# A graph network on one core: bucketed groups ordered in the first convolution go from 96 to 128, gathered groups of the first and third from 92 and 64 to 64 and 20

## The chip, the cores and the metric

One Trainium2 chip, one of its cores. The metric is the device time of one execution in microseconds (us). The kernel was written by hand, engine by engine, with its own semaphores; nothing is scheduled by a compiler.

## What is computed

A graph of 12,500 nodes with 32 features and 200,000 edges that come sorted by destination. First a layer of edge messages: each edge takes the 32 features of its source (`h`, a layer norm with a ReLU), a small network of the edge's weight and its direction, and the messages are summed by destination. Then three graph convolutions with widths 32, 128 and 32:

```
def _gcn_conv(x, src, dst, norm, W, b, n_nodes):
    h = x @ W
    msg = h[src] * norm[:, None]
    out = jax.ops.segment_sum(msg, dst, num_segments=n_nodes)
    return out + b
...
h = jnp.maximum(_layernorm(x, axis=-1), 0.0)
x = x + _L0_gnn_ref(h, edge_weight, edge_attr_3, edge_index, ...)
h = jnp.maximum(_layernorm(x, axis=-1), 0.0)
h = relu(_gcn_conv(h, src, dst, norm, W1, b1, n))
h = relu(_gcn_conv(h, src, dst, norm, W2, b2, n))
h = relu(_gcn_conv(h, src, dst, norm, W3, b3, n))
x = x + h
```

What costs time is `h[src]` followed by the sum over `dst`, four times over the 200,000 edges.

## The kernel before

The stages run one after the other, each after a table of node rows has been written to HBM: layer 0 (0 to 2664 us of the profile), preparation, the first convolution from 2771 us (called conv1), the second from about 4080 us (conv2), the third from 5526 us (conv3). Each has two ways of doing an edge, and splits its edges between them.

**A gathered group** is 1024 edges. POOL issues eight indirect DMAs (`gathers`, L782), each of 128 rows of the table, and behind each a memset of a scrap tile, 128x512 (`pause_between`, L762), for which the next gather waits (`made`). PE multiplies the rows by a one-hot matrix (L2153, `gathered_sum`, in eight matmuls for the convolutions), DVE adds the sum to the accumulator (L1766) and makes the next one-hot (L1657). Four groups can be in flight (`rows`), a buffer comes free when its sum has been made. Layer 0 gathers all of its 196 groups (`NG`).

**A bucketed group** is 1408 edges, ordered beforehand by the block of 128 nodes that the source lies in. It is done in `NCK` = 5 chunks, without any gather: the table lies in SBUF, and a chunk picks rows by matmuls with a one-hot of the sources. A chunk is: mark the sources (conv3: DVE L1613, `mark_sources`; conv1: ACT in two steps, L985 `near` and L994, for four chunks of five, and DVE L1613 for the fifth), PE `take` L2067 (20 matmuls), ACT `copy_bucket` L1007 (PSUM to SBUF), DVE `mark_destinations` L1642, PE `give` L2085 (5 matmuls). Each half of the marks waits until the take two chunks earlier is done (`bucket_taken`). Once for each group there is DVE `pair_destinations` L1624, DVE `add_bucket` L1726, and ACT's DMA `load_places` L968, 800 KB from HBM spread over all partitions, two groups ahead in conv3 (issued behind the last chunk's copy), one group ahead in conv1.

**Ordering.** Where an edge of a bucketed group belongs is found once, in conv1, for all groups that any convolution buckets (`NBG` = 96); the result goes to `places_d` in HBM and `dst_at` in SBUF, and conv2 and conv3 reuse it. One ordering is: DVE `count_blocks` L1543 to L1551, PE `count_prefix` L2040 (11 matmuls), ACT `copy_prefix` L976, DVE `rank_edges` L1557 to L1566, DVE `set_values` L1574 to L1580, PE `place_values` L2049 (44 matmuls), DVE `keep_places` L1587 to L1593, ACT's DMA `store_places` L958. Its parts are laid between the chunks of conv1 by hand: `parts_in(k, last)` says which part of which ordering goes with chunk k.

Tables of numbers set the mix: `GATHERED` gives the gathered groups of each stage, `LOOP` the gathered and bucketed groups of one iteration of each stage's loop, `REST` those of its last iteration. Before, conv1 gathers 92 groups and buckets 76 (380 chunks), conv2 100 and 70, conv3 64 and 96 (480 chunks). An iteration of conv1 has 50 chunks and 12 orderings (`RANKS`); an ordering takes four chunks there, and three in the last iteration, with parts in this order:

```
def parts_in(k, last):
    if last:
        return [divmod(k, 3)]
    return [(k // 4, (0, None, 1, 2)[k % 4])]
```

Two of the orderings stand ahead of conv1.

Of the kernel before, what the change touches and what calls it, by code (L numbers as in the profile page):

```python
# [27 lines left out]
P = 128  # L28
# [11 lines left out]
UNROLL = 4  # L40
# [27 lines left out]
GATHERED = [NG, 92, 100, 64]  # L68
LOOP = [(UNROLL, 0), (12, 10), (12, 8), (8, 12)]
REST = [(UNROLL, 0), (8, 6), (16, 14), (8, 12)]  # L70
# [21 lines left out]
RANKS = 12  # L92
# [15 lines left out]
assert RANKS % SLOTS == 0 and 4 * RANKS + 2 <= LOOP[1][1] * NCK and OWN_LAST == REST[1][1] - 2  # L108
assert OWN_LAST <= RANKS_LAST and 3 * RANKS_LAST == REST[1][1] * NCK

# [23 lines left out]
def gnn_kernel(nc, x, src, dst, edge_attr, edge_weight, w1, b1, w2, b2,  # L134
               W1, B1, W2, B2, W3, B3, out):
    ctx = ExitStack()
    with ctx:
# [59 lines left out]
        shared = sb("shared", [P, 5792])  # L197
        hid = shared[:, 0:1024].rearrange("p (s q e) -> p s q e", s=2, q=TPG // 2)
# [13 lines left out]
        odd_src = shared[:, 896:896 + NBG * BJ]  # L212
        odd_dst = shared[:, 2016:2016 + NBG * BJ]
# [18 lines left out]
        thirds1 = arena[:, 4208:4208 + NB * F3 // 2].bitcast(bf16).rearrange("p (b f) -> p b f", f=F3)  # L232
        thirds3 = arena[:, :].bitcast(bf16).rearrange("p (b f) -> p b f", f=2 * HID)[:, :, 0:F3]
        thirds = [None, thirds1, None, thirds3]
        src_b = arena[:, 8912:8912 + NBG * BJ].bitcast(i32)
        dst_b = arena[:, 9968:9968 + NBG * BJ].bitcast(i32)
        dst_b_rows = arena[0:NBG, 11024:11024 + BE].bitcast(i32)
        start_b = arena[:, 12432:12432 + NBG].bitcast(i32)
        src_place = arena[:, 9968:9968 + NBG * BJ].bitcast(bf16).rearrange("p (e two) -> p e two", two=2)
        dst_b_near = arena[:, 11024:11024 + NBG * BJ].bitcast(bf16).rearrange("p (e two) -> p e two", two=2)  # L240
        part_a = arena[:, 0:NBG * BJ].bitcast(i32)
        part_b = arena[:, 1120:1120 + NBG * BJ].bitcast(i32)
        near = arena[:, 1120:1120 + NBG * BJ]
# [288 lines left out]
        def parts_in(k, last):  # L532

            if last:
                return [divmod(k, 3)]
            return [(k // 4, (0, None, 1, 2)[k % 4])]
# [278 lines left out]
        def _(act):  # L815
# [201 lines left out]
            def conv(n):  # L1017

                def body(step, first, last):
                    groups, chunks_, starts_at = shape(n, last)  # L1020
                    u = -1
                    for k in range(chunks_):
# [15 lines left out]
                        for i, part in parts:  # L1038
                            if part == 1 and not last and i < RANKS:
                                copy_prefix(step, i)  # L1040
# [6 lines left out]
                        for i, part in parts:  # L1047
                            if part == 1 and last:
                                copy_prefix(step, i)
                            if part == (2 if last else None) and 0 < i <= (RANKS_LAST if last else RANKS):  # L1050
                                store_places(step, i - 1, last)
# [1231 lines left out]
```

How the kernel before makes its waits and increments, by code:

```python
        @block.sync  # L583
        def _(sp):
            for h, lo, hi in ((0, 0, 96), (0, 96, NB), (1, 0, 96), (1, 96, NB - 1)):
                sp.dma_start(dst_rows[lo:hi, h, :],
                             dst[(h * NB + lo) * GE:(h * NB + hi) * GE].rearrange("(g e) -> g e", e=GE)).then_inc(rows_in, 16)
            for at, n in ((0, ETAIL), (ETAIL, HALF - ETAIL), (HALF, HALF)):
                sp.dma_start(dst_rows[NB - 1:NB, 1, at:at + n],
                             dst[E - n:E].rearrange("(g e) -> g e", g=1)).then_inc(rows_in, 16)
            sp.dma_start(xn[:, 0:NB - 1, :], x[0:NCOL, :].rearrange("(p b) f -> p b f", p=P)).then_inc(x_in, 16)
            sp.wait_ge(pads, 1)
            sp.dma_start(xn[0:N - NCOL, NB - 1, :], x[NCOL:N, :]).then_inc(x_in, 16)
            def groups_of(lo, hi):
                return edge_attr[lo * GE:hi * GE, :].rearrange("(g e) c -> g (e c)", e=GE)
            for h, lo, hi in ((0, 0, 96), (0, 96, NB), (1, 0, 96)):
                sp.dma_start(attr_rows[lo:hi, h, :], groups_of(h * NB + lo, h * NB + hi)).then_inc(edges_in, 16)
            sp.wait_ge(pads, 2)
            sp.dma_start(attr_rows[96:NB - 1, 1, :], groups_of(NB + 96, NG - 1)).then_inc(edges_in, 16)
            sp.dma_start(attr_rows[NB - 1:NB, 1, 0:3 * ETAIL],
                         edge_attr[(NG - 1) * GE:E, :].rearrange("(g e) c -> g (e c)", g=1)).then_inc(edges_in, 16)
            sp.wait_ge(made, 9)
            sp.wait_ge(meta_ready, 2)
```

## Time and profile before

| | us |
|---|---|
| median of 3 runs (6437.45 to 6447.65) | 6441.06 |
| the profiled execution | 6419.31 |
| its span in the trace | 6417.5 |
| conv1, first to last `take` | 2770.7 to 3994.0 |
| conv3, first to last `take` | 5526.0 to 6391.9 |

Busy time over the span: POOL 5536.7 us (86%), PE 4556.8 (71%), DVE 3632.7 (57%), ACT 2714.1 (42%). The shares are averages over stages with different limits, so the views by stage and the single rows of a timeline say more. In a timeline a row is the start in us, the length in us, the engine, the line of the kernel, the operation with its tiles, and in brackets how long the engine had stood idle before it and what released it.

### The profile page before, as it was taken

What the parts mean: (1) busy time and instruction counts of PE and PEld (TensorE: products, weight loads), DVE (VectorE), ACT (ScalarE), POOL (GpSimd) and SP (SyncE); (2) the same over time, 40 slices, a digit from 0 to 9 for tenths busy, and PEclk for the clock granted to TensorE, in tenths of its full rate; (3) what the DMA queues carried; (4) which work ended last, traced back from release to release, by engine and by line L of the source; (5) the groups of instructions that cost most, each with busy time, mean ns of one, the idle gap of its engine ahead of it and who ended that gap; (6) DMA issues with size and microseconds to landing.
All of it is one profiled execution on the core that took longest, in us unless ns stands there. A gap on an engine that the chain in (4) does not pass through costs nothing.

```text
span 6417.5 us, 179150 instructions
## 1 busy us (share of the span) xinstructions
PE 4556.8 (71%) x62463; PEld 3336.9 (52%) x62464; DVE 3632.7 (57%) x8469; ACT 2714.1 (42%) x6550; POOL 5536.7 (86%) x7276
## 2 busy tenths in 40 slices
PE   4777777777777777655555555888888889766666
PEld 3444444444444444444444444777777778455554
DVE  7666666666666666755555555333333333544445
ACT  4444444444444444365555554333333344433332
POOL 7888888888888888588888887798888898688887
PEclk9888888888888888755555555888888899655555
DMA  3111111111111111332222222322222222433333
GB/s 79 31 30 30 30 30 30 30 30 30 30 30 30 30 30 30 34 75 69 64 69 69 69 69 70 96 81 76 81 81 76 81 81 85 118 105 109 110 107 98
DMA packets 494970, 400.88 MB, mean 62 GB/s; under 512 B 269575, under 2 KB 454828, under 8 KB 493537
## 3 DMA queue, kind: packets, MB, share of 16 engines
q10 hardware_dynamic: 146996, 207.67, 9.8%
q0 software_dynamic: 115712, 109.02, 9.7%
q1 hardware_dynamic: 231536, 74.48, 5.4%
q8 instruction: 459, 7.52, 0.5%
q14 instruction: 267, 2.19, 0.1%
HBM read 375.52 MB, written 15.29 MB: 61 GB/s over the span
## 4 chain that ended last, share of the span: by engine, by line
POOL 59%; issue 35%; POOLq 2%; PE 2%; DVE 1%; DMA 1%; ACT 0%; DVEq 0%; SPq 0%; ACTq 0%
POOL pause L762 31%; POOL rows L782 28%; POOLq L761 2%; PE radial L2209 0%; DMA table<-arena 0%; PE radial L2067 0%; PE radial L2222 0%; PE psX L2082 0%; POOLq L760 0%; PE sums L2153 0%; DMA rows<-table,idx 0%; DMA xn<-in_x 0%; DVE rows L1827 0%; PE radial L2008 0%; ACT rows L1103 0%
## 5 line engine op out<-in xcount | busy, mean ns | idle before, releaser
L782 POOL DMA_INDIRECT rows<-table,idx x3616 | 3535.1, 978 | 794.6 <-POOL pause L762 484.5
L762 POOL MEMSET pause<- 128x512 f32 x3616 | 1983.8, 549 | 2.5
L2067 PE MATMUL radial<-arena,shared 128*32 128x96 bf16 (+1 forms) x31200 | 1021.7, 277 | 198.9 <-issue 95.2
L1942 PEld LDWEIGHTS sums<-scratch,onehot 128*64 128x64 f32 x9408 | 791.4, 147 | 492.6 <-issue 205.5
L1942 PE MATMUL sums<-scratch,onehot 128*64 128x264 f32 (+1 forms) x9408 | 1009.1, 362 | 25.2 <-DVE scratch L1377 14.1
L2067 PEld LDWEIGHTS radial<-arena,shared 128*32 128x32 bf16 (+1 forms) x31200 | 719.2, 119 | 378.5 <-issue 169.5
L1007 ACT CAST scratch<-radial 128x480 bf16<-128x480 f32 x860 | 477.6, 557 | 985.4 <-PE radial L2067 750.1
L1924 PE MATMUL radial<-shared 64*128 64x384 bf16 x1568 | 296.8, 370 | 704.5 <-DVE scratch L1360 590.9
L1927 PE MATMUL radial<-shared 64*128 64x384 f32 x3136 | 785.6, 582 | 0.0
L2153 PE MATMUL sums<-onehot,rows 128*128 128x80 f32 (+1 forms) x2844 | 402.3, 314 | 515.8 <-DMA rows<-table,idx 489.2
L1360 DVE TENSOR_TENSOR scratch<-radial,shared 128x768 f32<-128x768 f32 x784 | 743.6, 949 | 0.0
L1613 DVE TENSOR_SCALAR shared<-scratch,line 128x640 bf16<-128x640 bf16 (+1 forms) x906 | 455.3, 503 | 480.5 <-PE radial L2067 387.4
L880 ACT COPY shared<-rows 128x192 f32<-128x192 f32 x196 | 89.3, 456 | 1494.4 <-DMA rows<-table,idx 1493.1
L2153 PEld LDWEIGHTS sums<-onehot,rows 128*128 128x128 f32 (+1 forms) x2844 | 365.5, 223 | 569.0 <-issue 566.2
L850 ACT ACTIVATE dist<-iota,rel 128x64 f32<-128x64 f32 (+1 forms) x2368 | 620.3, 344 | 34.4 <-issue 31.9
L1326 DVE TENSOR_TENSOR shared<-arena,rows 128x576 f32<-128x576 f32 x196 | 148.7, 759 | 755.6 <-ACT shared L887 446.7
L1766 DVE TENSOR_TENSOR accT<-accT,sums 96x80 f32 (+1 forms) x256 | 60.3, 236 | 897.1 <-PE sums L2153 723.9
L1924 PEld LDWEIGHTS radial<-shared 64*128 64x128 bf16 x1568 | 82.4, 95 | 931.2 <-issue 711.3
L1352 DVE TENSOR_TENSOR scratch<-radial,shared 128x512 f32<-128x512 f32 x784 | 535.3, 683 | 13.4 <-issue 13.4
L1003 ACT COPY scratch<-radial 128x384 f32<-128x384 f32 x350 | 167.8, 480 | 589.7 <-PE radial L2067 585.3
L1642 DVE TENSOR_TENSOR shared<-radial,shared 128x480 bf16<-128x480 bf16 x860 | 344.0, 401 | 50.1 <-PE psT L2085 17.6
L1927 PEld LDWEIGHTS radial<-shared 64*128 64x128 f32 x3136 | 337.9, 222 | 36.9 <-issue 31.0
(237 smaller groups left out, 6075.3 us busy)
## 6 DMA issues: line engine op xcount, KB each, us to landing
scratch<-places_d ACTq DMA_DIRECT2D x242, 800.0 KB
rows<-table,idx POOLq DMA_INDIRECT x3616
shared<-in_edge_weight SPq DMA_DIRECT2D x390, 128.0 KB
idx<-in_src SPq DMA_DIRECT2D x451, 4.0 KB
table<-arena SPq DMA_DIRECT2D x24, 256.0 KB, 2.5
table<-arena SPq DMA_DIRECT2D x2, 1176.0 KB, 10.6
accT<-in_edge_attr SPq DMA_DIRECT2D x2, 1152.0 KB
table<-arena SPq DMA_DIRECT2D x24, 96.0 KB, 2.0
```

The lines of the kernel that those rows point to most:

```text
L762: nc.gpsimd.memset(pause[:, :], 0.0).then_inc(made, 1)
L782: (pool.indirect_dma_start(rows_3[:, r, j, :] if n in (1, 3) else rows[:, r, j, 0:WIDTH[n]], None, tables[n], bass.IndirectOffsetOnAxis(ap ...
L850: ins = nc.scalar.activation(dist[:, j, 0:span], iota[:, 0:span], ACT.Abs, scale=-1.0, bias=rel[:, bass.ds(step.tile(u) + j, 1)])
L1007: nc.scalar.copy(taken[n][:, h, :, :], radial[0][:, h, 0:KC * F3].rearrange("p (t f) -> p t f", f=F3)).then_inc(bucket_copied, 1)
L1352: prod = v.tensor_tensor(msg[:, h, t:t + 2, 0:2 * SEG0].rearrange("p t (m s) -> p t m s", s=16), R[:, :, 0:256].rearrange("p t (m s) -> p ...
L1360: last = v.tensor_tensor(msg[:, h, t:t + 2, SEG0 + 16 * (MUL + 1):TAIL0].rearrange("p t (n s) -> p t n s", s=16), R[:, :, 256:384].unsquee ...
L1613: v.tensor_scalar(from_src[n][:, k % 2, :, :, :], places[v_ % 2][:, :, c * KC * CAP:(c + 1) * KC * CAP].rearrange("p i (t r) -> p i t r", ...
L1924: nc.tensor.matmul(radial[q % 2][:, k, 0:RDIM], ones_h[half, :], bias_rows[half, :], start=True, stop=False, tile_position=(k * HID0, 0))
L1927: last = nc.tensor.matmul(radial[q % 2][:, k, 0:RDIM], hid[half, u % 2, q, :], w2n[half, 0, :], start=False, stop=True, tile_position=(k * ...
L1942: last = nc.tensor.matmul(there, onehot[:, u % 2, 4 * h + t, 0:SW], taken_from, start=(h + q + part == 0), stop=(h == 1 and q == 1 and par ...
L2067: last = nc.tensor.matmul(d, from_src[n][:, h, i, t, :], table_of(n, s), start=True, stop=True, tile_position=(0, 32 * i))
L2153: mm = nc.tensor.matmul(sums[0:w, u % 2, 0:CWIN], far_rows[j], (onehot if n == 2 else onehot_3)[0:counts[j], u % 2, j, 0:CWIN], start=(j = ...
```

## The change

1. The third convolution gathers 20 groups and buckets 128 (640 chunks), in 5 iterations, not 8: 160 gathers in it for 512.
2. The first convolution gathers 64 groups and buckets 96 (480 chunks): 512 gathers for 736. All 3616 gathers become 3040. Layer 0 and the second convolution keep their numbers.
3. `NBG` follows the largest number of buckets: 128 groups are ordered, 126 of them within conv1 (before 94). Every iteration now uses the order that the last one had, an ordering in three chunks with a part in each; an iteration of conv1 has 60 chunks and 16 orderings, the last one 14 orderings in 60 chunks. 378 of the 480 chunks carry a part.
4. ACT's `copy_prefix` stands behind the copy of its chunk in all iterations; before, it stood between the two marking steps in all but the last.
```diff
-GATHERED = [NG, 92, 100, 64]
-LOOP = [(UNROLL, 0), (12, 10), (12, 8), (8, 12)]
-REST = [(UNROLL, 0), (8, 6), (16, 14), (8, 12)]
+GATHERED = [NG, 64, 100, 20]
+LOOP = [(UNROLL, 0), (8, 12), (12, 8), (4, 26)]
+REST = [(UNROLL, 0), (8, 12), (16, 14), (4, 24)]
...
-RANKS = 12
+RANKS = 16
...
+        bucket_edges = sb("bucket_edges", [P, 2 * NBG * BJ])
...
-        odd_src = shared[:, 896:896 + NBG * BJ]
-        odd_dst = shared[:, 2016:2016 + NBG * BJ]
+        odd_src = shared[:, 1024:1024 + NBG * BJ]
+        odd_dst = bucket_edges[:, NBG * BJ:2 * NBG * BJ]
...
         def parts_in(k, last):
 
-            if last:
-                return [divmod(k, 3)]
-            return [(k // 4, (0, None, 1, 2)[k % 4])]
+            return [divmod(k, 3)]
...
                         parts = parts_in(k, last) if n == 1 else []
-                        for i, part in parts:
-                            if part == 1 and not last and i < RANKS:
-                                copy_prefix(step, i)
                         if n == 1 and more and (k + 1) % NCK != NCK - 1:
                             mark_sources(step, k + 1)
                         copy_bucket(n, step, k)
...
                         for i, part in parts:
-                            if part == 1 and last:
+                            if part == 1 and i < (RANKS_LAST if last else RANKS):
                                 copy_prefix(step, i)
-                            if part == (2 if last else None) and 0 < i <= (RANKS_LAST if last else RANKS):
+                            if part == 2 and 0 < i <= (RANKS_LAST if last else RANKS):
                                 store_places(step, i - 1, last)
...
-    nc = bacc.Bacc("TRN2", target_bir_lowering=False, num_devices=1)
+    nc = bacc.Bacc("TRN2", target_bir_lowering=False, num_devices=1, dynamic_dma_scratch_size=4096)
```

How the instructions move is shown for two engines in the first loop body of conv1. ACT before, over the four chunks of one ordering (`places_d` holds the places in HBM, `scratch<-radial 128x480` is the copy of a chunk, `arena<-radial 128x104` is `copy_prefix`):

```order
L968 DMA scratch<-places_d 128x4x800 [waits places_out1]
L985 ACTIVATE shared<-scratch,line 128x640 [waits bucket_taken]
L976 CAST arena<-radial 128x104 [waits prefix_made]
L994 ACTIVATE shared<-shared,one 128x640 [waits from_src_near]
L1007 CAST scratch<-radial 128x480 [waits bucket_summed,bucket_taken] x2
L985 ACTIVATE shared<-scratch,line 128x640 [waits bucket_taken,places_in1]
L994 ACTIVATE shared<-shared,one 128x640 [waits from_src_near]
L1007 CAST scratch<-radial 128x480 [waits bucket_summed,bucket_taken]
L985 ACTIVATE shared<-scratch,line 128x640 [waits bucket_taken]
L994 ACTIVATE shared<-shared,one 128x640 [waits from_src_near]
L1007 CAST scratch<-radial 128x480 [waits bucket_summed,bucket_taken]
L958 DMA places_d<-src_at 128x32 [waits src_at_made]
```

ACT in the change, over the three chunks of one ordering (its lines are one lower):

```order
L1006 CAST scratch<-radial 128x480 [waits bucket_summed,bucket_taken]
L967 DMA scratch<-places_d 128x4x800 [waits places_out1]
L984 ACTIVATE shared<-scratch,line 128x640 [waits bucket_taken]
L993 ACTIVATE shared<-shared,one 128x640 [waits from_src_near]
L1006 CAST scratch<-radial 128x480 [waits bucket_summed,bucket_taken]
L975 CAST arena<-radial 128x104 [waits prefix_made]
L1006 CAST scratch<-radial 128x480 [waits bucket_summed,bucket_taken]
L957 DMA places_d<-src_at 128x32 [waits src_at_made]
L984 ACTIVATE shared<-scratch,line 128x640 [waits bucket_taken,places_in1]
L993 ACTIVATE shared<-shared,one 128x640 [waits from_src_near]
L1006 CAST scratch<-radial 128x480 [waits bucket_summed,bucket_taken]
```

`copy_prefix` went from between the two marking steps to behind the copy of its chunk, and the store of the places comes once in three copies, not once in four.

DVE before, from `count_blocks` to the start of `rank_edges` (L1642 is `mark_destinations`, once for each chunk):

```order
L1543 TENSOR_TENSOR arena<-radial,arena 128x1144 [waits places_summed]
L1546 TENSOR_TENSOR arena<-arena 128x121
L1549 TENSOR_TENSOR arena<-arena 128x121 [waits ranking]
L1551 TENSOR_REDUCE arena<-arena 128x11 [waits ranking]
L1642 TENSOR_TENSOR shared<-radial,shared 128x480
L1642 TENSOR_TENSOR shared<-radial,shared 128x480 [waits bucket_summed]
L1557 TENSOR_TENSOR arena<-arena 128x1144 [waits prefix_copied]
```

DVE in the change (its lines are four lower):

```order
L1539 TENSOR_TENSOR arena<-radial,arena 128x1144 [waits places_summed]
L1542 TENSOR_TENSOR arena<-arena 128x121
L1545 TENSOR_TENSOR arena<-arena 128x121 [waits ranking]
L1547 TENSOR_REDUCE arena<-arena 128x11 [waits ranking]
L1638 TENSOR_TENSOR shared<-radial,shared 128x480 [waits bucket_summed,dst_paired]
L1553 TENSOR_TENSOR arena<-arena 128x1144 [waits prefix_copied]
```

One chunk's `mark_destinations` now stands between the two steps, where there were two.

## Rows read from the trace of the kernel before

**Rows 1.** Windows: layer 0, conv1, conv3; length, busy of each engine, PEclk, DMA.

```profile
95.00:2664.00 2569.00, 1884.34 (x14035) 1158.29 (x14033) 1790.78 (x3460) 1055.89 (x3074) 2300.09 (x3071) 0.88 0.17 31
2735.00:3997.00 1262.00, 707.17 (x15491) 543.78 (x15489) 728.10 (x2413) 711.52 (x1093) 1114.99 (x1472) 0.52 0.27 67
...
5520.00:6390.00 870.00, 581.96 (x12453) 449.37 (x12452) 429.32 (x1339) 268.78 (x484) 777.19 (x1016) 0.52 0.38 106
```

**Rows 2.** Timeline of POOL in layer 0, two gathers, a pause left out.

```profile
395.78 0.95 POOL L782 DMA_INDIRECT rows<-table,idx  x1 [0.16 <-POOL pause L762]
...
398.76 1.06 POOL L782 DMA_INDIRECT rows<-table,idx  x1 [1.48 <-issue]
```

**Rows 3.** The chain between 230 and 900 us: start, us, what.

```profile
397.28 1.26 issue
...
557.65 1.27 issue
```

**Rows 4.** Waits of conv3 for gathered rows: us in total, times, longest.

```profile
PE sums L2153 <- DMA rows<-table,idx: 99.4, 40, 6.6
```

**Rows 5.** One line, the takes of conv1, then of conv3: count, first and last start.

```profile
L2067 PE MATMUL radial<-arena,shared x7600: 202/281/281, 2770.7 to 3994.0; 128*32 128x96 bf16 x195
...
L2067 PE MATMUL radial<-arena,shared x9600: 202/281/281, 5526.0 to 6391.9; 128*32 128x96 bf16 x196
```

**Rows 6.** Timeline of ACT in conv3, while POOL gathers.

```profile
5916.10 0.56 ACT L1007 CAST scratch<-radial 128x480 bf16<-128x480 f32 x1 [1.12 <-PE radial L2067]
5917.78 0.56 ACT L1007 CAST scratch<-radial 128x480 bf16<-128x480 f32 x1 [1.12 <-PE radial L2067]
5919.45 0.56 ACT L1007 CAST scratch<-radial 128x480 bf16<-128x480 f32 x1 [1.11 <-PE radial L2067]
```

**Rows 7.** Timeline of POOL over the same time.

```profile
5915.53 0.55 POOL L762 MEMSET pause<- 128x512 f32 x1
...
5917.32 0.54 POOL L762 MEMSET pause<- 128x512 f32 x1
...
5918.99 0.54 POOL L762 MEMSET pause<- 128x512 f32 x1
```

**Rows 8.** Timeline of PE in conv3, when POOL has ended its last gather.

```profile
6387.31 0.59 PE L2067 MATMUL radial<-arena,shared 128*32 128x96 bf16 x20
...
6388.39 0.59 PE L2067 MATMUL radial<-arena,shared 128*32 128x96 bf16 x20
...
6391.08 0.40 PE L2067 MATMUL radial<-arena,shared 128*32 128x96 bf16 x20
...
6391.76 0.40 PE L2067 MATMUL radial<-arena,shared 128*32 128x96 bf16 x20
```

**Rows 9.** Groups of conv3 by line and form, DVE: count, busy, mean ns.

```profile
L1613 DVE TENSOR_SCALAR shared<-scratch,line 128x640 bf16<-128x640 bf16 x478 | 204.6, 428 | 212.2 <-PE radial L2067 152.2 <-remote 44.8 <-issue 12.4
L1642 DVE TENSOR_TENSOR shared<-radial,shared 128x480 bf16<-128x480 bf16 x477 | 191.0, 400 | 33.0 <-PE psT L2085 17.6 <-PE psX L2085 12.2 <-remote 2.9
```

**Rows 10.** Timeline of ACT in conv1, a load of places and who waits for it.

```profile
3489.27 0.41 ACTq L968 DMA_DIRECT2D scratch<-places_d  x1
...
3493.47 0.83 ACT L985 ACTIVATE shared<-scratch,line 128x640 bf16<-128x640 bf16 x1 [0.38 <-DMA scratch<-places_d]
```

**Rows 11.** Timeline of DVE in conv1, last iteration: starts of orderings.

```profile
3897.36 0.74 DVE L1543 TENSOR_TENSOR arena<-radial,arena 128x1144 bf16<-128x1144 bf16 x1
...
3904.76 0.75 DVE L1543 TENSOR_TENSOR arena<-radial,arena 128x1144 bf16<-128x1144 bf16 x1
...
3917.97 0.75 DVE L1543 TENSOR_TENSOR arena<-radial,arena 128x1144 bf16<-128x1144 bf16 x1
...
3926.67 0.75 DVE L1543 TENSOR_TENSOR arena<-radial,arena 128x1144 bf16<-128x1144 bf16 x1
```

**Rows 12.** Timeline of ACT in conv1, two copies with no ordering between them.

```profile
2797.41 0.56 ACT L1007 CAST scratch<-radial 128x480 bf16<-128x480 f32 x1
...
2799.47 0.54 ACT L1007 CAST scratch<-radial 128x480 bf16<-128x480 f32 x1
```

More of the change, by code:

```diff
@@ L107 @@
 RANKS_LAST = OWN_LAST + OTHERS - (RANKS - OWN) * (ITS[1] - 1)
-assert RANKS % SLOTS == 0 and 4 * RANKS + 2 <= LOOP[1][1] * NCK and OWN_LAST == REST[1][1] - 2
-assert OWN_LAST <= RANKS_LAST and 3 * RANKS_LAST == REST[1][1] * NCK
+assert RANKS % SLOTS == 0 and 3 * RANKS + 3 <= LOOP[1][1] * NCK and OWN_LAST == REST[1][1] - 2
+assert OWN_LAST <= RANKS_LAST and 3 * RANKS_LAST <= REST[1][1] * NCK
 NORM0 = sqrt(4 * pi) / sqrt(2 * MUL)
@@ L229, in gnn_kernel @@
         taken = [None, taken_3, taken_w, taken_3]
-        thirds1 = arena[:, 4208:4208 + NB * F3 // 2].bitcast(bf16).rearrange("p (b f) -> p b f", f=F3)
+        thirds1 = arena[:, 4320:4320 + NB * F3 // 2].bitcast(bf16).rearrange("p (b f) -> p b f", f=F3)
         thirds3 = arena[:, :].bitcast(bf16).rearrange("p (b f) -> p b f", f=2 * HID)[:, :, 0:F3]
         thirds = [None, thirds1, None, thirds3]
[L235 to L240, printed above, removed]
+        src_b = bucket_edges[:, 0:NBG * BJ].bitcast(i32)
+        dst_b = arena[:, 9600:9600 + NBG * BJ].bitcast(i32)
+        dst_b_rows = arena[0:NBG, 11008:11008 + BE].bitcast(i32)
+        start_b = arena[:, 12416:12416 + NBG].bitcast(i32)
+        src_place = arena[:, 9600:9600 + NBG * BJ].bitcast(bf16).rearrange("p (e two) -> p e two", two=2)
+        dst_b_near = arena[:, 11008:11008 + NBG * BJ].bitcast(bf16).rearrange("p (e two) -> p e two", two=2)
         part_a = arena[:, 0:NBG * BJ].bitcast(i32)
-        part_b = arena[:, 1120:1120 + NBG * BJ].bitcast(i32)
-        near = arena[:, 1120:1120 + NBG * BJ]
+        part_b = arena[:, 1408:1408 + NBG * BJ].bitcast(i32)
+        near = arena[:, 1408:1408 + NBG * BJ]
         in_block = arena[:, 0:BJ * NCODE // 2].bitcast(bf16).rearrange("p (j c) -> p j c", j=BJ)
@@ L1055, in body @@
                             load_places(n, step, v + 2)
-                    if last and n == 1:
+                    if last and n == 1 and 3 * RANKS_LAST + 2 >= chunks_:
                         store_places(step, RANKS_LAST - 1, last)
@@ L1778, in body @@
                             ranking(step, k, last)
-                    if last and n == 1:
+                    if last and n == 1 and 3 * RANKS_LAST >= chunks_:
                         keep_places(step, RANKS_LAST - 1, last)
@@ L2182, in body @@
                         turn_given(step, chunks_ // NCK - 1)
-                    if last and n == 1:
+                    if last and n == 1 and 3 * RANKS_LAST >= chunks_:
                         place_values(step, RANKS_LAST - 1)
```

## The prediction, made before the changed kernel had run

> **What bounds the kernel now.** I cut the span into its stages first, with the windows, since the page's shares average over them. In layer 0 POOL is busy 2300 of 2569 us, in conv1 1115 of 1262, in conv3 777 of 870 [rows 1]. POOL's timeline gives its beat: a gather of 0.95 us, 0.16 us of idle time ahead of it [rows 2], and a pause memset of 0.54. In conv3 the pauses start 1.79 and 1.67 us apart [rows 7]; over the stage 1.69 us (866 us for 512 gathers), 13.5 for a group of eight. Every 96th gather is late: POOL stands idle for 1.48 us where it stands 0.16 otherwise [rows 2], and the chain shows two such stretches of 1.27 us 160.3 us apart, which is 96 beats [rows 3]. In conv3 PE waits for gathered rows 40 times, 99.4 us in all [rows 4]. So conv1 and conv3 cost what their gathers cost: conv3's takes span 5526.0 to 6391.9, 866 us for 512 gathers; conv1's 2770.7 to 3994.0, 1223 us for 736 [rows 5].
>
> The second thing to see is the pace of a bucketed chunk. While POOL gathers, conv3's copies start 1.68 and 1.67 us apart [rows 6], and each starts just when a pause memset ends on POOL: 5915.53 plus 0.55 is 5916.08, the copy starts at 5916.10; 5917.32 plus 0.54 is 5917.86, copy 5917.78; 5918.99 plus 0.54 is 5919.53, copy 5919.45 [rows 7]. I read this as a lock: the end of a take becomes visible once in a beat of POOL. When POOL has issued its last gather the takes follow one another in 1.08 us with matmuls at the half clock (0.59 us a take) and then in 0.68 us at 0.40 us a take [rows 8]. The clock granted over conv1 and conv3 is 0.52 of full speed, so nearly always the 1.2 GHz level; in layer 0 it is 0.88 [rows 1].
>
> **The change, part by part.** Durations are those of the profiled execution, 6419.3 us; the median shown is 21.8 us above it, so the sum is a difference, added to 6441.06.
>
> **conv3.** It loses 352 gathers and gets 160 chunks. 20 groups at 13.5 us keep POOL busy for 270 us. In that time chunks go at 1.69 us: 160 chunks. The other 480 run unlocked. Their lower bound is the tail's fastest pace, taken as 0.76 (a little over the 0.68 seen) [rows 8]; the upper is its cold pace, 1.09. Two more floors lie between. DVE needs 0.43 for the marks of the sources and 0.40 for those of the destinations [rows 9], 0.83 us, and two small operations for each group (some 0.25 us each, over five chunks) make it about 0.92 us a chunk. And the load of places (L968): in conv1 one was issued at 3489.27 and its user released at 3493.47, 4.2 us [rows 10]. In conv3 it is issued behind the last copy of one group and used six takes later; with mark and take some 5.5 us in six chunks, 0.92 us again. I take **1.0 us**: both floors, and a clock that is high most of the time. 270 + 480 = 750 us for 866: **-116**. Ends: at 0.76 635 us, -231; at 1.09 793 us, -73. The waits for rows of gathers should go, since a group then comes every 32 chunks and four can be in flight.
>
> **conv1.** It loses 224 gathers, gets 100 chunks and 32 orderings. 64 groups at 13.5 us are 864 us, so POOL no longer sets its length: the chunks with their orderings do. The new order is the one that the last iteration had, so its rows price it: `count_blocks` starts at 3897.36 and again at 3904.76, 7.4 us, with no gather waited for; 3917.97 to 3926.67, 8.7 us, holds a wait for one [rows 11]. I take 8.0 us, between them. 126 orderings are 1008 us. The other 102 chunks go at ACT's pace, two copies 2.06 us apart [rows 12], 209 us. 1217 for 1223: -6. In the order of ACT, `copy_prefix` moves behind a copy, some 1.4 us later than between the marks; DVE has one `mark_destinations` between `count_blocks` and `rank_edges` in place of two. Both are within the last iteration's rows already. The tables for 128 groups make preparation a little longer, DVE operations of a third more columns ahead of the first chunk; I put +3. Together **-3**; ends 7.4 us (-79) and 8.7 us (+85).
>
> **Descriptor scratch.** It is a quarter. If the late gather every 96th is the recycling of this space, it comes every 24th. Where POOL bounds (layer 0 and conv2, 2368 gathers) there were 24 such stalls of 1.32 us, 32 us. Four times as many at a quarter of the length each is **0**; at the same length, 72 more, +95; if a short one hides in the 0.16 us between, -32. Elsewhere POOL has slack, and it costs nothing.
>
> **Layer 0, conv2, the tables between:** not touched, 0. Sum: -116 - 3 + 0 = **-119**, 6441 - 119 = **6322 us**.
>
> **The rivals.**
>
> *A: the stall keeps its length.* For it: its length is the same to 0.01 us both times [rows 3], as a fixed piece of work or a wait for one landing would be. Against it: a walk over 96 entries would be constant too. +95: 6417 us, within a few us of the edge of no change.
>
> *B: the clock stays at 1.2 GHz in conv3.* For it: 0.52 over the stage [rows 1], and 1.08 us between takes in each burst before the clock rises. Against it: PE had waits in nearly every chunk there, and it rose after PE had run three takes without one [rows 8]. 270 + 523 = 793 us, so -73 and -3: 6365 us. The Trainium skill (TensorE: Matmul & The Clock Gate, "What's actually happening") says that the default is throttled and that activity releases it; by that rule B falls, the trace's tail agrees with it (0.59 us a take becomes 0.40), and the forecast stands.
>
> *C: the ordering in each chunk is the new chain of conv1, and B holds too.* An ordering runs through DVE, PE, ACT, DVE, PE and DVE again, each step behind a chunk's own work. If three chunks need 8.7 us always [rows 11], conv1 is +85; with -73 the sum is +12: 6453 us, near no change, and with part of A's 95 clearly slower. It decides from 8.6 us an ordering.
>
> *D, the other side: the pace of 1.69 us is the chunk's own.* The place is the loop take, copy, give, marks of conv3; the lock to POOL would be by chance of equal lengths. For it: 1.68 us stands in every row of the stage [rows 6], and gathers that wait for sums could take their beat from the chunks. Against it: the tail's 1.08 and 0.68 [rows 8]. Price: 640 x 1.69 = 1082 us for 866, +216, with conv1's -3: 6654 us. It decides from a pace of 1.35 us, where 640 chunks last 866. A rule speaks on its side. The Trainium skill (SBUF — State Buffer, "Who interferes with whom") says that PE and ACT never wait on anyone; by it POOL's work could not hold back the end of a take, and the time would be D's 6654. The rows of POOL and ACT side by side [rows 6, 7] are against the rule here, as far as three beats can be.
>
> **How the numbers follow.** Forecast as it stands 0.43, A 0.24, B 0.14, C 0.11, D 0.08. A measurement of this kernel tells about 0.2%, 13 us, from no change. Faster: the forecast, B, and 0.14 of A: 0.71. Same: 0.06, of A. Slower: D, C, and 0.04 of A: 0.23. The range goes from 6200, the forecast with conv3 at its warm pace (-118), to 6540, C with the whole of A's 95; outside lie D and the lowest corner of all ends.
>
> **What would show it.** In the changed kernel's profile: 3040 gathers; conv3's takes spanning about 750 us; copies 1.69 us apart only while POOL has gathers and about 1.0 apart else; PEclk high in conv3; waits of PE for gathered rows near nothing; POOL idle in conv3 two thirds of the time. conv1's takes spanning about 1217 us with `count_blocks` every 8.0 us. Late gathers every 24th, of 0.3 us each beyond the 0.16. The forecast is wrong if copies of conv3 stay 1.6 us apart with POOL idle (D), if late gathers keep 1.48 us (A), if takes stay at 0.59 us (B), if conv1 is over 1290 us long (C).

## The result, and the profile after

The changed kernel takes **6186.68 us** (median of 4 runs, 6179.96 to 6193.57); the kernel before, timed beside it, 6439.26 us (4 runs). The ratio is **0.9608, 95% interval 0.9591 to 0.9626**, so 252.6 us less, where 119 were forecast (6322, range 6200 to 6540). The direction was right, the size less than half, and the time lies below the range.

The page of the changed kernel (its profiled execution took 6193.57 us), with the span, the busy times, three rows of the slices and the shares of the chain by engine and by line:

```profile
span 6191.7 us, 194777 instructions
...
PE 4635.9 (75%) x70151; PEld 3410.8 (55%) x70152; DVE 3941.3 (64%) x9309; ACT 2973.3 (48%) x7002; POOL 4661.6 (75%) x6124
...
PE   4777777777777777756666666788888888988787
...
POOL 7999999999999999947666666298988889863330
PEclk9888888888888888865555555688888889988877
...
POOL 40%; issue 27%; DVE 11%; PE 10%; DMA 6%; ACT 2%; POOLq 1%; DVEq 1%; SPq 0%; ACTq 0%
POOL pause L761 21%; POOL rows L781 19%; DMA scratch<-places_d 5%; PE radial L2063 3%; PE radial L2036 2%; DVE arena L1553 1%; PE psX L2081 1%; PE psT L2081 1%; PE radial L2045 1%; POOLq L760 1%; DVE arena L1539 1%; DVE arena L1556 1%; DVE arena L1560 1%; DVE shared L1609 1%; DVE shared L1638 1%
```

POOL is at 4661.6 us where it was at 5536.7; its digits are still 9 in layer 0 and mostly 8 and 9 in the second convolution, and they fall to 3 and 0 in the last four slices, the third convolution. The clock row, 5 in those slices before, is now at 8 and 7. The windows of layer 0, the first and the third convolution, to lay beside [rows 1]:

```profile
95.00:2664.00 2569.00, 1899.03 (x14187) 1167.19 (x14186) 1807.82 (x3499) 1057.67 (x3088) 2296.30 (x3075) 0.89 0.17 31
2740.00:3960.00 1220.00, 811.98 (x19444) 640.56 (x19444) 911.48 (x2985) 869.26 (x1374) 747.96 (x994) 0.51 0.29 80
5480.00:6170.00 690.00, 560.66 (x16168) 426.62 (x16172) 522.06 (x1599) 357.41 (x641) 238.30 (x308) 0.81 0.49 159
```

In the third convolution PE is busy 561 of 690 us and DVE 522; POOL only 238. The granted clock is 0.81 of full speed where it was 0.52. The first convolution stays at 0.51. The takes of the first and then of the third convolution, beside [rows 5]:

```profile
L2063 PE MATMUL radial<-arena,shared x9600: 206/281/281, 2747.5 to 3952.8; 128*32 128x96 bf16 x196
```

```profile
L2063 PE MATMUL radial<-arena,shared x12800: 202/206/281, 5481.9 to 6165.5; 128*32 128x96 bf16 x197
```

By these rows the stages compare as follows. The last column is the prediction's term.

| from first to last take, us | before | after | measured | forecast |
|---|---|---|---|---|
| all ahead of the first convolution | 2770.7 | 2747.5 | -23.2 | +3 |
| first convolution | 1223.3 | 1205.3 | -18.0 | -6 |
| from there to the third | 1532.0 | 1529.1 | -2.9 | 0 |
| third convolution | 865.9 | 683.6 | -182.3 | -116 |
| sum over the spans (with the last 26 us) | 6417.5 | 6191.7 | -225.8 | -119 |

The spans differ by 226 us and the medians by 253: the profiled execution of before was 20 us faster than the median of its runs, that of after 7 us slower. So 107 us of the forecast's error lie in the stages, and 27 in which execution was profiled. Of the 107, 66 are the third convolution's, 26 lie ahead of the first (layer 0's gathers alone span 26.6 us less, 2605.7 for 2632.3), 12 in the first and 3 between it and the third.

Layer 0's gathers, at the place where one stood idle for 1.48 us before [rows 2]:

```profile
396.03 0.95 POOL L781 DMA_INDIRECT rows<-table,idx  x1 [0.16 <-POOL pause L761]
...
397.68 0.95 POOL L781 DMA_INDIRECT rows<-table,idx  x1 [0.16 <-POOL pause L761]
...
399.33 0.95 POOL L781 DMA_INDIRECT rows<-table,idx  x1 [0.16 <-POOL pause L761]
```

There is no late gather any more: beyond the first 32 of layer 0's 1568 gathers the old trace has one every 96th, 15 of them (the expectations below say 16), that starts 2.98 us after the one before it, 1.33 us more than the median beat. Over the whole kernel there are 31, 15 in layer 0 and 6, 6 and 4 in the convolutions. The new trace has none. And the waits of the third convolution, beside [rows 4]:

```profile
ACT scratch L1006 <- PE radial L2063: 314.9, 531, 5.2
POOL rows L781 <- PE sums L2149: 279.9, 13, 27.2
...
DVE shared L1609 <- DMA scratch<-places_d: 60.4, 66, 2.7
...
PE sums L2149 <- DMA rows<-table,idx: 1.0, 1, 1.0
```

PE waits once, 1.0 us, for gathered rows (40 times, 99.4 us before). POOL waits instead, 280 us in 13 stretches, for sums that free its buffers. New is a wait of DVE for the loads of places, 66 times, 60 us.

The last thing is the pace of a chunk. Copies of the third convolution in the changed kernel, and POOL's gathers over the same time:

```profile
5658.24 0.56 ACT L1006 CAST scratch<-radial 128x480 bf16<-128x480 f32 x1 [2.62 <-PE radial L2063]
...
5659.35 0.56 ACT L1006 CAST scratch<-radial 128x480 bf16<-128x480 f32 x1 [0.55 <-PE radial L2063]
5660.44 0.56 ACT L1006 CAST scratch<-radial 128x480 bf16<-128x480 f32 x1 [0.53 <-PE radial L2063]
5661.61 0.56 ACT L1006 CAST scratch<-radial 128x480 bf16<-128x480 f32 x1 [0.61 <-PE radial L2063]
```

```profile
5658.01 0.95 POOL L781 DMA_INDIRECT rows<-table,idx  x1 [0.16 <-POOL pause L761]
...
5659.72 0.96 POOL L781 DMA_INDIRECT rows<-table,idx  x1 [0.16 <-POOL pause L761]
...
5661.38 0.95 POOL L781 DMA_INDIRECT rows<-table,idx  x1 [0.16 <-POOL pause L761]
```

POOL is gathering, and the copies come 1.11, 1.09 and 1.17 us apart, at no fixed place of its beat (5658.24 is 0.23 us behind the start of a gather, 5659.35 is 1.34 behind it, 5660.44 is 0.72 behind the next). Counted over the stage, the takes follow one another in 1.07 us on average while POOL gathers (235 of them) and in 1.07 us while it doesn't (404). The 1.69 us that the prediction charged to 160 chunks don't exist here.

### The profile page after: what moved, and what is told of

Read it like the earlier page. It is cut to its first block, busy times and chain, and to the rows that moved or that the text cites. A ratio compares the mean times of both kernels' runs of the same rounds, so it can differ in the third digit from the quotient of the medians.

```text
span 6191.7 us, 194777 instructions
## 1 busy us (share of the span) xinstructions
PE 4635.9 (75%) x70151; PEld 3410.8 (55%) x70152; DVE 3941.3 (64%) x9309; ACT 2973.3 (48%) x7002; POOL 4661.6 (75%) x6124
## 4 chain that ended last, share of the span: by engine, by line
POOL 40%; issue 27%; DVE 11%; PE 10%; DMA 6%; ACT 2%; POOLq 1%; DVEq 1%; SPq 0%; ACTq 0%
POOL pause L761 21%; POOL rows L781 19%; DMA scratch<-places_d 5%; PE radial L2063 3%; PE radial L2036 2%; DVE arena L1553 1%; PE psX L2081 1%; PE psT L2081 1%; PE radial L2045 1%; POOLq L760 1%; DVE arena L1539 1%; DVE arena L1556 1%; DVE arena L1560 1%; DVE shared L1609 1%; DVE shared L1638 1%
## 5 line engine op out<-in xcount | busy, mean ns | idle before, releaser
L781 POOL DMA_INDIRECT rows<-table,idx x3040 | 2944.3, 969 | 1308.1 <-PE sums L2149 607.3
L761 POOL MEMSET pause<- 128x512 f32 x3040 | 1698.7, 559 | 1.7
L2063 PE MATMUL radial<-arena,shared 128*32 128x96 bf16 (+1 forms) x36400 | 1062.6, 263 | 333.3 <-ACT shared L993 164.9
L1006 ACT CAST scratch<-radial 128x480 bf16<-128x480 f32 x1120 | 618.4, 552 | 421.9 <-PE radial L2063 407.6
L1609 DVE TENSOR_SCALAR shared<-scratch,line 128x640 bf16<-128x640 bf16 (+1 forms) x1086 | 570.0, 525 | 263.2 <-PE radial L2063 164.0
L1348 DVE TENSOR_TENSOR scratch<-radial,shared 128x512 f32<-128x512 f32 x784 | 535.0, 682 | 13.7 <-issue 13.5
L1638 DVE TENSOR_TENSOR shared<-radial,shared 128x480 bf16<-128x480 bf16 x1120 | 448.4, 400 | 96.0 <-PE psX L2081 44.0
L2149 PE MATMUL sums<-onehot,rows 128*128 128x80 f32 (+1 forms) x2272 | 337.1, 319 | 210.4 <-DMA rows<-table,idx 195.3
L2149 PEld LDWEIGHTS sums<-onehot,rows 128*128 128x128 f32 (+1 forms) x2272 | 308.7, 227 | 248.4 <-issue 242.1
L1762 DVE TENSOR_TENSOR accT<-accT,sums 128x80 f32 (+1 forms) x184 | 43.2, 235 | 610.1 <-PE sums L2149 601.2
L984 ACT ACTIVATE shared<-scratch,line 128x640 bf16<-128x640 bf16 x384 | 318.1, 828 | 83.3 <-DMA scratch<-places_d 57.5
```

The source lines that it names most:

```text
L761: nc.gpsimd.memset(pause[:, :], 0.0).then_inc(made, 1)
L781: (pool.indirect_dma_start(rows_3[:, r, j, :] if n in (1, 3) else rows[:, r, j, 0:WIDTH[n]], None, tables[n], bass.IndirectOffsetOnAxis(ap ...
L1006: nc.scalar.copy(taken[n][:, h, :, :], radial[0][:, h, 0:KC * F3].rearrange("p (t f) -> p t f", f=F3)).then_inc(bucket_copied, 1)
L1348: prod = v.tensor_tensor(msg[:, h, t:t + 2, 0:2 * SEG0].rearrange("p t (m s) -> p t m s", s=16), R[:, :, 0:256].rearrange("p t (m s) -> p ...
L1609: v.tensor_scalar(from_src[n][:, k % 2, :, :, :], places[v_ % 2][:, :, c * KC * CAP:(c + 1) * KC * CAP].rearrange("p i (t r) -> p i t r", ...
L1638: v.tensor_tensor(by_twos(to_dst[n][:, k % 2, :, :]), row_pairs(iota1_ps, KC), in_pairs(dst_pair[:, v_ % 2, c * KC:(c + 1) * KC, :], BWIN) ...
```

## The experiments

Three things were to be explained: why chunks beside gathers are no longer slow, where the late gathers went, and how much of the gain is the scratch, the first and the third convolution. The theories at the start were S, that the smaller descriptor scratch did both of the first two, and M, that the mix of groups did. The runs are called e1 to e13 (there is no e4), as in the expectations. All ratios are to the kernel before, timed beside each run; e6, e7 and e9 were executed once each.

### The scratch alone

```diff
-    nc = bacc.Bacc("TRN2", target_bir_lowering=False, num_devices=1)
+    nc = bacc.Bacc("TRN2", target_bir_lowering=False, num_devices=1, dynamic_dma_scratch_size=4096)
```

> The kernel before with the descriptor scratch of the change (4096), nothing else. Theory S (the scratch did it): the late gathers of every 96th (1.48 us of idle time) are gone in all stages, as in the changed kernel, which is 16 x 1.33 us in layer 0 and 8 x 1.3 in the second convolution, and the copies of the third convolution follow their takes within 0.1 us, where they came 0.3 to 1.6 us late; as POOL still bounds each stage the time falls by about 30 to 45 us, to some 6400. Theory M (the mix did it, the scratch does nothing): the profile is that of before, late gathers and late copies included, 6440. Rival A of the prediction (the stall comes four times as often at its full length): 6535.

Measured (e1): 6385.5 us for 6428.8, ratio 0.9930 (0.9913 to 0.9947). The late gathers are gone in all stages, layer 0's gathers span 2605.6 us (before 2632.3, after 2605.7). In the third convolution 337 of 474 copies beside gathers start within 0.1 us of their take's last matmul and none later than 0.3, where the trace of before had 32 of 471 within 0.1 us and 269 over 1.3 us late. That looked like theory S in full, though the stage was only 7.6 us shorter (858.4). The time fits the stalls: 31 x 1.33 = 41 us, measured 43. Rival A is out: no stall came back more often.

### Size of the scratch or place of the tiles

```diff
+        room = sb("room", [P, 3072])
         accT = sb("accT", [P, NPAD + WIN])
...
+    nc = bacc.Bacc("TRN2", target_bir_lowering=False, num_devices=1, dynamic_dma_scratch_size=4096)
```

> The kernel before with the descriptor scratch at 4096, as in e1, and an unused tile of 12,288 bytes for each partition ahead of all others, so that every tile lies where it lay before. If the size of the scratch is what counts, the run is e1's: copies of the third convolution within 0.3 us of their takes, no gather late every 96th, 6385 us. If it was the place of the tiles, the copies are 0.3 to 1.6 us late as before and the time is 6430.

Measured (e5): 6385.4 us, ratio 0.9927 (0.9910 to 0.9943), copies on time, no late gather. So where the tiles lie shows no effect; the size of the scratch takes the late gathers away. (The copies need more than that, see below.) How it goes with the size was tried with 8192 on the kernel before:

> The kernel before with half of its descriptor scratch (8192). With 16384 layer 0 has 16 late gathers, 96 apart, each 1.33 us longer than the median; with 4096 and 2048 it has none. If the late gather is the reuse of the whole scratch and each quarter of it hides in the beat, half of it may show as gathers 48 apart, up to 33 of them of 0.5 us or less extra: 6385 to 6405. If the length of a late gather doesn't depend on the size, it comes twice as often: 33 of 1.33 us in layer 0, 6455. If it is only 16384 that has it, 6385 and no gather over 2.2 us beyond the first 32.

e12 took 6384.0 us, ratio 0.9921 (0.9905 to 0.9938), and in layer 0 no two gathers start over 2.2 us apart beyond the first 32. Of the sizes 16384, 8192 and 4096 only the first has late gathers. They don't scale with the size, and what they are stays open. Then the changed kernel, with only the size set to 2048:

> The changed kernel with half of its descriptor scratch (2048 for 4096). If a smaller scratch only makes the recycling finer, so that each piece hides behind the pause, the time stays at 6187 and no gather is late. If the scratch holds too few descriptors for the gathers that are in flight, POOL waits at each of them for a landing: gathers of layer 0 come more than 1.65 us apart and the time is over 6250.

e2 took 6173.3 us, ratio 0.9598 (0.9582 to 0.9614) against the kernel before, where the changed kernel had 0.9608 with an overlapping interval: no difference shown, layer 0 the same to 1 us.

### The state that the prediction summed

The third convolution beside few gathers, with the full scratch and then with the small one. Both leave out 44 gathered groups of it:

```diff
-GATHERED = [NG, 92, 100, 64]
-LOOP = [(UNROLL, 0), (12, 10), (12, 8), (8, 12)]
-REST = [(UNROLL, 0), (8, 6), (16, 14), (8, 12)]
+GATHERED = [NG, 92, 100, 20]
+LOOP = [(UNROLL, 0), (12, 10), (12, 8), (4, 20)]
+REST = [(UNROLL, 0), (8, 6), (16, 14), (4, 16)]
...
-E0 = GATHERED[3] * GE
+E0 = 64 * GE
...
-BUCKETED = [0] + [NBG - (GATHERED[n] * GE - E0) // BE for n in (1, 2, 3)]
+BUCKETED = [0] + [NBG - (GATHERED[n] * GE - E0) // BE for n in (1, 2)] + [NBG]
```

> The kernel before, full scratch, with the third convolution at 20 gathered and 96 bucketed groups; the other 44 gathered groups are left out, their edges are not computed. This is the state that the prediction summed, 480 chunks beside 160 gathers with the full scratch. By the prediction's terms 160 chunks go at 1.69 us while POOL gathers and 320 at 1.0: its takes span 590 us, with the copies late while POOL gathers and on time else. If the pace of 1.69 us is the chunks' own (rival D) they span 810 us. If the full scratch does no harm to a stage that is not bound by gathers, they span 480 x 1.07 = 513 us.

> e6 with the scratch at 4096, the same 44 gathered groups of the third convolution left out. With the pace of the changed kernel, 683.5 us for 640 chunks, its takes span 513 us, all copies within 0.3 us of their takes. The difference to e6 is what the full scratch costs a stage whose gathers do not bound it: 77 us by the prediction's terms, 0 if late copies cost nothing there.

Their takes, in e6 and then in e7:

```profile
L2067 PE MATMUL radial<-arena,shared x9600: 202/206/281, 5551.7 to 6046.4; 128*32 128x96 bf16 x196
```

```profile
L2067 PE MATMUL radial<-arena,shared x9600: 202/206/281, 5510.8 to 6010.3; 128*32 128x96 bf16 x196
```

Measured: **494.7 us with the full scratch (e6), 499.6 with the small one (e7)**, for 480 chunks. Neither 590 nor 810; 1.03 and 1.04 us a chunk, with 1.02 and 1.03 beside gathers, and all but three of the 960 copies within 0.3 us of their takes. The full scratch doesn't slow the chunks. That is against theory S: the first convolution of this kernel is the same program as before, with the same scratch, and there 140 of 371 copies beside gathers are within 0.1 us, where the trace that I had read has 8 of 373.

### The first convolution with both scratches

Once with the changed kernel's code and scratch (e3: the third convolution back at 64 and 96, 96 groups ordered), once the same with the tiles and the scratch of before (e8). The edit of e3, against the changed kernel:

```diff
-GATHERED = [NG, 64, 100, 20]
-LOOP = [(UNROLL, 0), (8, 12), (12, 8), (4, 26)]
-REST = [(UNROLL, 0), (8, 12), (16, 14), (4, 24)]
+GATHERED = [NG, 64, 100, 64]
+LOOP = [(UNROLL, 0), (8, 12), (12, 8), (8, 12)]
+REST = [(UNROLL, 0), (8, 12), (16, 14), (8, 12)]
...
-RANKS = 16
+RANKS = 12
```

> The change without its third convolution: the first takes 64 gathered and 96 bucketed groups, the third stays at 64 and 96, 96 groups are ordered (12 orderings in each iteration of 60 chunks, at three chunks each), scratch 4096. If the third convolution's time hangs on its gathers, its takes span the 866 us of before, less at most 10. The first convolution has 94 orderings: at the 8.0 us of the prediction 752 us and 198 chunks at 2.05 us, 406 us, so 1158 us where before had 1223 and the change 1205. With layer 0 and the second convolution shorter by 30 us the sum is 6441 - 65 - 30 = about 6345. If the orderings cost nothing beyond their chunks the first convolution is at its gathers, 64 x 13.5 = 864 us, or at 480 chunks x 2.05 = 984 us: then 6170.

e3 took 6284.7 us, ratio 0.9776 (0.9760 to 0.9793). The third convolution takes 858.5 us, still at its gathers, as expected. The first takes 1121.6 us, 36 less than the 1158 of the prediction's prices, and the run 60 less than the 6345 expected. Within an iteration `count_blocks` comes every 7.9 us (mean of 86 distances), so it is less the ordering that was priced too high than the chunks without one: (1121.6 - 94 x 7.9) / 198 = 1.9 us for 2.05.

> e3 (the first convolution with 64 gathered and 96 bucketed groups, the third as before, 96 groups ordered three chunks each) with the tiles and the full scratch of the kernel before. If the full scratch holds back the takes wherever POOL gathers, the first convolution is longer than e3's 1121.6 us, by 0.5 us or more a chunk while POOL is busy (some 860 us of it): 1200 us or over, and the run is at 6285 + 43 + 80 = about 6410. If not, only the late gathers come back: 1122 us and about 6320.

e8 took 6313.2 us, ratio 0.9817 (0.9801 to 0.9833), as the second expectation has it. The first convolution takes 1122.6 us: the 80 us that the full scratch was to cost are not there. The late gathers are back, and again the copies of the third convolution are on time (358 of 470 within 0.1 us). Now only one trace had late copies in the third convolution: that of before.

### The kernel before, profiled once more

> The kernel before, unchanged, profiled once more. The full scratch alone does not make copies late (e6, whose first convolution is this same code, had 140 of 371 within 0.1 us, the first profile 8 of 373). If the late copies belong to the one execution that the prediction read, this profile has the copies of the third convolution within 0.3 us of their takes, while its takes still span about 866 us, since the gathers bound them, and PE then waits for gathered rows well over the 99 us of the first profile. If they belong to this kernel's mix of gathers and chunks, they are 0.3 to 1.6 us late again.

This execution (e9) took 6435.6 us. The wait of PE for gathered rows over the third convolution:

```profile
PE sums L2153 <- DMA rows<-table,idx: 299.7, 64, 6.5
```

64 waits for 64 groups, 299.7 us, three times what [rows 4] shows. ACT's copies, and PE around a gathered group:

```profile
5914.79 0.56 ACT L1007 CAST scratch<-radial 128x480 bf16<-128x480 f32 x1 [0.54 <-PE radial L2067]
5915.94 0.56 ACT L1007 CAST scratch<-radial 128x480 bf16<-128x480 f32 x1 [0.59 <-PE radial L2067]
5916.97 0.56 ACT L1007 CAST scratch<-radial 128x480 bf16<-128x480 f32 x1 [0.47 <-PE radial L2067]
5918.12 0.56 ACT L1007 CAST scratch<-radial 128x480 bf16<-128x480 f32 x1 [0.59 <-PE radial L2067]
5919.14 0.56 ACT L1007 CAST scratch<-radial 128x480 bf16<-128x480 f32 x1 [0.47 <-PE radial L2067]
...
5920.23 0.56 ACT L1007 CAST scratch<-radial 128x480 bf16<-128x480 f32 x1 [0.53 <-PE radial L2067]
5927.20 0.56 ACT L1007 CAST scratch<-radial 128x480 bf16<-128x480 f32 x1 [6.42 <-PE radial L2067]
```

```profile
5919.58 0.59 PE L2067 MATMUL radial<-arena,shared 128*32 128x96 bf16 x20
5925.38 0.83 PE L2153 MATMUL sums<-onehot,rows 128*96 128x80 bf16 x8 [5.21 <-DMA rows<-table,idx]
```

Between two groups the copies come 1.02 to 1.15 us apart, while POOL gathers all the time, and then PE waits 5.21 us for the next group's rows. The median distance of two takes is 1.09 us; in the first trace it was 1.65. The stage's takes span the same: 865.1 us and 866.0, since the gathers set it either way. The window, beside the last of [rows 1]:

```profile
5520.00:6390.00 870.00, 516.97 (x12294) 408.80 (x12291) 443.90 (x1325) 275.77 (x501) 774.75 (x1018) 0.64 0.37 106
```

PE is busy 517 us (582 in the first trace), at a clock of 0.64 (0.52). The stage lies 16 us later in this trace; over its own takes, 5542 to 6408, it is 514.5 us at 0.65. So the slow, even pace belonged to **one execution**, in which the slack ahead of each group was spread over the chunks.

In that execution the lock was no accident of three rows. Of its 480 copies in the third convolution 415 start more than 0.3 us late, and 376 of these start 1.3 to 1.7 us after the start of a gather, around the end of the pause. In e9 one copy is over 0.3 us late, and the starts are spread over the whole beat (135 of 480 in that stretch). What made the copies late was not found; the same program showed nothing of it in this profile, nor in the first convolution of e6. Nor does it show in the four times of the changed kernel: 160 chunks at 1.69 us for 1.07 would be some 100 us, and they lie within 14 us. One more number sets that execution apart: its granted clock over the whole span is 0.759, where e9 has 0.782 and the 28 timed runs of the kernel before beside e1 to e13 have 0.780 to 0.787. As far as that marks the lock, it came once in 30 executions, and it cost nothing: 6419.3 us is the shortest of them all.

The 31 late gathers are in both traces, at the same places. The first and the second convolution are longer in e9, takes of 1232.1 and 1427.3 us for 1223.3 and 1410.7. So the stage table holds to some 10 or 20 us a row: beside e9 the first convolution would have lost 26.8 us, and the stretch from it to the third 17.5.

### The floor of the third convolution

```diff
+                        v, c = divmod(k, NCK)
+                        if n > 1 and c == NCK - 1 and not (last and k + 2 * NCK >= chunks_):
+                            act.wait_ge(*sources_made(n, step, k))
+                            load_places(n, step, v + 2)
                         copy_bucket(n, step, k)
-                        v, c = divmod(k, NCK)
...
-                        if n > 1 and c == NCK - 1 and not (last and k + 2 * NCK >= chunks_):
-                            load_places(n, step, v + 2)
```

> The changed kernel with the load of a group's places issued ahead of the last copy of the group two before it, behind a wait for that chunk's marks, in the second and third convolutions. In the changed kernel's third convolution DVE waits 66 times, 60 us in all, for these loads. If the load is one of the floors of the chunks' pace, most of these waits go and the third convolution's takes span 640 to 660 us where they spanned 683.5, the run 6150 to 6165. If DVE's own 0.92 us a chunk or PE's clock holds the pace, the waits move elsewhere and the time stays.

This is e11. It took 6198.4 us, ratio 0.9627 (0.9611 to 0.9643), no gain; the third convolution's takes span 685.2 us (683.5). The wait did go:

```profile
DVE shared L1610 <- DMA scratch<-places_d: 8.0, 14, 1.7
```

8 us where there were 60. The time didn't follow, so the load was not the floor. Which of DVE (busy 522 us for 640 chunks, 0.82 us each) and PE's clock holds the pace of 1.07 was not tried apart. The profiles of this stage give a hint only, its takes beside its granted clock:

| run | takes, us | clock |
|---|---|---|
| changed kernel | 683.5 | 0.81 |
| e11 | 685.2 | 0.84 |
| e13 | 661.0 | 0.85 |
| e2 | 662.7 | 0.86 |
| e10 | 656.6 | 0.87 |

The two at the lower clocks are the longest. As e2 differs from the changed kernel in the scratch alone, 20 us more or less in this stage say nothing about an edit.

### The pause, and a faster version

The chain of the changed kernel gives 21% to the pause. It was halved in the changed kernel:

```diff
-PAUSE = 512
+PAUSE = 256
```

> The changed kernel with a pause memset of 128x256 in place of 128x512. If POOL's own work bounds layer 0 and the second convolution, the beat falls from 1.65 to about 1.38 us and layer 0's gathers span 2605 x 1.38 / 1.65 = 2180 us, the whole run about 500 us less, 5690. If the pause covers something that a gather needs (its descriptors' landing, or DVE's work beside it), the gathers themselves become longer by what the pause loses, and the time stays within 1% of 6187.

**e10 took 5779.2 us, ratio 0.8985 (0.8970 to 0.9000)**, where 5690 were expected. Layer 0's gathers span 2374.6 us (2605.7), the second convolution's takes 1259.7 (1410.1), the first's 1188.4 (1205.3), the third's 656.6 (683.5, but see e2 above). POOL in layer 0:

```profile
1000.60 0.95 POOL L781 DMA_INDIRECT rows<-table,idx  x1 [0.16 <-POOL pause L761]
1001.55 0.33 POOL L761 MEMSET pause<- 128x256 f32 x1
1002.04 0.95 POOL L781 DMA_INDIRECT rows<-table,idx  x1 [0.16 <-POOL pause L761]
...
1003.48 1.37 POOL L781 DMA_INDIRECT rows<-table,idx  x1 [0.16 <-POOL pause L761]
```

The pause is 0.21 us shorter and the median beat is 1.44 us; the mean beat is 1.515, where 1.38 were expected, since gathers took 1.02 us on average where they took 0.955. The long ones have fixed places: of 384 gathers over 1.05 us 374 are the third or the sixth of their group, as the last row. Why these two was not found. A quarter of the pause, with the scratch at 2048:

> The changed kernel with a pause of 128x128 and a scratch of 2048, in search of the fastest version. e10's half pause took 0.21 us off the pause and added 0.07 us to a gather: layer 0's beat fell from 1.66 to 1.515 us. If the pause goes on counting one for one, the beat falls by some 0.1 us more, 160 us in layer 0 and 80 in the second convolution, 5540. If other work bounds layer 0 next (DVE's 1806 us and PE's 1897 of 2565 are below it), or gathers get longer by what the pause loses, it stays at e10's 5779.

**e13 took 5438.5 us, ratio 0.8456 (0.8442 to 0.8470)**, the fastest version, where 5540 were expected: the gathers were back at 0.958 us, with 18 over 1.05, and the mean beat was 1.346. As e13 differs from e10 in pause and scratch, which of the two took the long gathers away is open.

```profile
1000.05 0.95 POOL L781 DMA_INDIRECT rows<-table,idx  x1 [0.16 <-POOL pause L761]
1001.00 0.22 POOL L761 MEMSET pause<- 128x128 f32 x1
1001.38 0.95 POOL L781 DMA_INDIRECT rows<-table,idx  x1 [0.16 <-POOL pause L761]
```

The window of layer 0, 2005 us of it:

```profile
95.00:2100.00 2005.00, 1663.08 (x13758) 1070.31 (x13758) 1751.36 (x3394) 1032.98 (x3009) 1761.44 (x3004) 1.00 0.19 38
```

DVE is busy 1751 us, POOL 1761, PE 1663 at full clock: now three engines stand close together. A next step would probably have to take from all of them; none was tried.

## Why the prediction was wrong, point by point

**What bounds the kernel: right.** POOL's gathers and pauses set layer 0, the second convolution, and the first and third as they were. For layer 0 and the second convolution the pause runs show it most plainly.

**The pace beside gathers: wrong, and the largest term.** The step that failed is "20 groups at 13.5 us keep POOL busy for 270 us. In that time chunks go at 1.69 us: 160 chunks", with its ground, "I read this as a lock". The chunks beside gathers measured 1.07 us. The prediction's 480 chunks at 1.0 us measured 1.07. So 640 x 1.07 = 683 us in place of 270 + 480 = 750: 66 us of the 107. The lock was there in the trace that was read, but in one execution, of a stage that is bound elsewhere. In such a stage a chunk can be spaced out up to the gathers' pace without the stage growing longer, so its spacing isn't its cost. Without the lock the same program spaces its chunks by 1.09 us (e9), and 480 chunks beside 20 gathered groups, the sum's own state, take 1.03 us each (e6). A better estimate was in the same rows, the pace of 1.08 us in the tail: 640 x 1.08 = 691 us. And the rows of the lock were read too kindly: two of the three copies start 0.08 us before the end of the pause that was to release them.

**The range's lower end** left out the combination of a fast third convolution with a gain from the scratch; the terms' own ends would have allowed it (-231 for the third convolution, -3 and -32 for the scratch give 6175), and 6200 was set above that by choice. Two sums beside the range are slightly off: the warm pace is 115 us below the forecast, not 118, and C with the whole of A's 95 is 6548, not 6540. Neither matters for the result.

**The scratch: term mis-sized, 0 for about -28.** The bound "if a short one hides", -32, was the right case; the stalls of the POOL-bound stages went altogether. Layer 0 and the second convolution had 21 of them, 21 x 1.33 = 28 us by estimate, where the prediction counted 24. On the kernel before, where all four stages wait for POOL, the scratch is worth more, in medians 43, 47 and 50 us (e1, e5, e12). With the first convolution off its gathers, e3 against e8, it is 0.0041 of the time, 26 us, each ratio known to 0.0017. The prediction's reason, a recycling whose pieces scale with the size, is not borne out: 8192 shows no late gather either.

**The first convolution: right within 12 us.** Forecast 126 x 8.0 + 102 x 2.05 = 1217 us, measured 1205.3, with `count_blocks` every 7.9 us within an iteration (mean of 118 distances). The two parts of it are larger than the difference: 28 gathered groups fewer, with 20 bucketed ones more and the new order of parts, gave 98 us (1219.9 in e1, 1121.6 in e3), 32 more orderings took 84 back (1205.3), 2.6 us each beyond their chunks. In e3 the same prices were 36 us too high, so part of the agreement here is luck.

**The rivals.** A (the stall keeps its length): in none of the ten profiles with a smaller scratch does a gather of layer 0, beyond the first 32, start over 2.2 us after the one before it. B (the clock stays down): no, the granted clock is 0.81 in the third convolution, so mostly the 2.4 GHz level, and the median matmul of its takes lasts 206 ns for 281. The Trainium skill's rule that activity releases the throttle (TensorE: Matmul & The Clock Gate, "What's actually happening") was on the right side, the trace agrees. C: no, 7.9 us an ordering, and it decides from 8.6. D (the pace is the chunk's own): no, 683.5 us and not 1082. But its witness deserves a word: the rule of the Trainium skill (SBUF — State Buffer, "Who interferes with whom") that PE and ACT never wait on anyone, said there of the ports of SBUF, was weighed against three beats of one trace and lost. The thirteen other profiles agree with it as far as they reach: in each, all but at most four of the 480 or 640 copies of the third convolution start within 0.3 us of their take's last matmul, also while POOL gathers. The first trace shows 415 late ones, and whether a port has anything to do with them no run here shows.

**The shares.** Going by the ratios (1, then 0.9930 with the scratch, 0.9776 with the first convolution too, 0.9608 with all) of 6439 us: some 45 us are the scratch, 99 the first convolution's mix, 108 the third's mix with the 32 orderings that it needs. The parts depend on this order: taken after the first convolution's mix, the scratch is worth 26 us, not 45.

## What to carry to other kernels

The spacing of work in a stage that something else bounds is slack and cost together, and it can differ from one execution to the next. Take its price from a burst after a wait, from a tail, or from a second profile, before it goes into a sum for a stage that it will bound. And where the chain of waits gives a fifth to one filler instruction, change that instruction's size first: here it was worth 750 us (6186.7 to 5438.5, with the scratch at 2048, which alone showed no difference), three times the change.

## What was not expected of the hardware

With a descriptor scratch of 16384 every 96th indirect DMA of this kernel starts 1.33 us late, with 8192, 4096 or 2048 none does; that is 0.7 to 0.8% of its time (e1, e5, e12). Indirect DMAs of 128 rows with a pause of 0.22 us between them ran at a beat of 1.35 us (e13), with the gather itself as long (0.96 us) as with a pause of 0.54. With 0.33 us it was 1.02 on average (e10), at another size of the scratch. And in one of two profiled executions of the same program ACT's copies fell in step with POOL's beat, without any cost in time.
